# Expert stage of a mixture-of-experts layer: VectorE writes the odd group's first bias row, GpSimd makes the scatter indices

## The reference

```
h  = x @ W1[e].T + b1[e]            # 512 numbers
a, b = split(h, 2)                  # 256 each
g  = a * sigmoid(b)
eo = g @ Wo.T + bo
out += eo * comb[e]                 # over the two chosen experts
```

## Time and profile before

| what | value |
|---|---|
| median of 3 runs | 716.66 us (714.81 to 716.93) |
| the profiled execution, its own time | 718.54 us |
| its span, first to last instruction | 716.8 us |
| granted TensorE clock, mean | 0.949 |
| instructions | 14297 |

### The profile page before, as it was taken

One profiled execution on the slowest core, in us unless ns is written; L12 is line 12 of the kernel. 1 busy time (PEld: TensorE's weight loads), 2 busy tenths in 40 slices (PEclk: granted clock), 3 DMA queues, 4 the chain that ended last, 5 costly groups with the idle time before them and its releaser, 6 DMA issues. The chain is left out here.

```text
span 716.8 us, 14297 instructions
## 1 busy us (share of the span) xinstructions
PE 618.1 (86%) x3515; PEld 470.7 (66%) x3515; DVE 602.6 (84%) x1384; ACT 522.4 (73%) x1321; POOL 536.9 (75%) x657
## 2 busy tenths in 40 slices
PE   3566789999999989989889777828999999999994
PEld 1433556667777667666667465615888888888883
DVE  6389999999999999997999846566788888888884
ACT  2666578898888957986856576644778878887883
POOL 5457667899999779899969884566588766666666
PEclk9989999999999999999999999957999999999997
DMA  4999888889998897898898799625465444444430
GB/s 109 259 140 133 118 115 134 134 141 157 153 139 155 132 139 121 149 169 148 156 148 151 142 266 290 246 97 152 130 98 86 81 82 81 76 84 80 83 60 1
DMA packets 103300, 95.58 MB, mean 133 GB/s; under 512 B 14523, under 2 KB 82710, under 8 KB 102966
## 3 DMA queue, kind: packets, MB, share of 16 engines
q1 hardware_dynamic: 85846, 79.69, 60.3%
q0 software_dynamic: 16176, 12.75, 9.6%
q10 hardware_dynamic: 1200, 2.23, 0.8%
HBM read 35.47 MB, written 25.61 MB: 85 GB/s over the span
## 5 line engine op out<-in xcount | busy, mean ns | idle before, releaser
L2065 POOL DMA_INDIRECT out<-res,index x91 | 141.4, 1553 | 56.4 <-DVE res L2150 36.5
L843 POOL TENSOR_TENSOR rs_prod<-rT,state_rows 128x512 f32<-128x512 f32 x128 | 139.3, 1097 | 41.0 <-DVE state_rows L1528 39.3
L1281 PEld LDWEIGHTS ps_k<-w,gel 128*128 128x128 f32 x512 | 61.4, 200 | 17.0 <-issue 13.2
L1989 ACT ACTIVATE sig<-ps_a 128x256 f32<-128x256 f32 x91 | 35.1, 385 | 42.8 <-DVE glu L2126 16.9
L1281 PE MATMUL ps_k<-w,gel 128*128 128x128 f32 x512 | 64.1, 286 | 2.4 <-ACT gel L1098 2.4
L1246 PE MATMUL ps_f<-hnT_hi,mix_hi 128*128 128x512 f32 x128 | 55.2, 431 | 8.4 <-DVE hnT_lo L1651 7.6
L2117 DVE SCALAR_TENSOR_TENSOR half<-ps_b,xg,sig 128x256 f32<-128x256 f32 x91 | 43.6, 479 | 21.4 <-ACT sig L1993 18.6
L2110 DVE SCALAR_TENSOR_TENSOR ps_a<-ps_a,xg,sig 128x256 f32<-128x256 f32 x91 | 44.4, 487 | 11.0 <-issue 7.5
L2015 ACT ACTIVATE ps_b<-bias_rows 128x512 f32 x89 | 53.0, 595 | 0.0
L1248 PE MATMUL ps_f<-hnT_hi,mix_lo 128*128 128x512 f32 x128 | 52.2, 408 | 0.0
L1247 PE MATMUL ps_f<-hnT_lo,mix_hi 128*128 128x512 f32 x128 | 52.1, 407 | 0.0
(11 more groups left out here) (357 smaller groups left out, 2000.6 us busy)
## 6 DMA issues: line engine op xcount, KB each, us to landing
v_spread<-vT SPq DMA_DIRECT2D x128, 256.0 KB, 5.3
xg<-sorted_scratch SPq DMA_DIRECT2D x91, 130.0 KB
xin<-in_L_attn_x SPq DMA_DIRECT2D x16, 256.0 KB, 6.3
x<-in_L_attn_x SPq DMA_DIRECT2D x16, 256.0 KB
out<-x SPq DMA_DIRECT2D x16, 256.0 KB
sorted_scratch<-gel SPq DMA_DIRECT2D x4, 910.0 KB, 8.0
tokens_scratch<-h SPq DMA_DIRECT2D x12, 256.0 KB
raw_w<-in_L_ffn_W ACTq DMA_DIRECT2D x2, 1024.0 KB, 9.3
```

Source lines behind the costliest of these rows:

```text
L843: pool.tensor_tensor(rs_prod[:, p, idx % 4], rT[p][:], state[idx][:, p * NT:(p + 1) * NT], ALU.mult).then_inc(s["rs_ready"], 1)
L1281: mm = pe.matmul(ps_k2[:, q * P:(q + 1) * P], gel[c][:, q * P:(q + 1) * P], w2[:, c, :], start=(c == 0), stop=(c == NF - 1))
L2065: pool.indirect_dma_start(out_rows, bass.IndirectOffsetOnAxis(ap=index[k % RESULTS][:, i:i + 1], axis=0), res[k % RESULTS][:, i, :], None, ...
```

## The change

VectorE, in its iteration `k`, reads the low expert of group 2k + 3 from `pair_table` into a register at the head of the iteration (`low_of`), and after `join(2k+1)` copies that expert's bias row into the bank `ps_a` of the odd group 2k + 3 (`odd_seed`). TensorE then no longer does the bias product for odd groups from the fourth on, but waits for the copy (`odd_seeded`). GpSimd makes the row numbers of two pairs at once (`number`) into one tile `index`, before the scatters of every second iteration, with waits for the input (`xT_ps`) and for the older scatters (`stored`); `finish` on VectorE no longer makes them.

```diff
-                if j < FIRST_SEED or i == 1:
+                if j < FIRST_SEED:
                     bias(ps_a[j % 2], low)
+                elif i == 1:
+                    pe.wait_ge(s["odd_seeded"], k - FIRST_SEED // 2 + 1)
                 else:
                     pe.wait_ge(s["low_seeded"], k - FIRST_SEED // 2 + 1)
...
             def scatter(k, i):
                 j = 2 * k + i
                 pool.wait_ge(s["res_ready"], k + 1)
+                pool.wait_ge(s["numbered"], k // 2 + 1)
...
+            def number(m):
+
+                first, end = 4 * m, min(4 * m + 4, GROUPS)
+                n, columns = end - first, slice(first % (2 * RESULTS), first % (2 * RESULTS) + end - first)
+                for k in range(2 * m, (end + 1) // 2):
+                    pool.wait_ge(s["xT_ps"], k + 1)
+                    if k >= RESULTS:
+                        pool.wait_ge(s["stored"][k % RESULTS], 16 * count_to(k - RESULTS, RESULTS))
+                rows = xg[:, slot(first):slot(first) + n, TAGS + ID:TAGS + ID + 1].rearrange("p i c -> p (i c)")
+                if first >= early_groups:
+                    left = left_out[:, first - early_groups:end - early_groups]
+                    if first == early_groups:
+                        pool.wait_ge(s["left_set"], 1)
+                    pool.tensor_tensor(left, rows, left, ALU.add).then_inc(s["summed"], 1)
+                    pool.wait_ge(s["summed"], m - early_groups // 4 + 1)
+                    rows = left
+                pool.tensor_copy(index[:, columns], rows).then_inc(s["numbered"], 1)
...
             for k in range(PAIRS):
+                if k % 2 == 0:
+                    number(k // 2)
                 if k >= 1:
                     scatter(k - 1, 0)
                     scatter(k - 1, 1)
...
+            def low_of(j):
+
+                if not FIRST_SEED <= j < GROUPS:
+                    return None
+                if j == early_groups + 1:
+                    dve.wait_ge(s["tables_set"], 1)
+                both = dve.value_load(pair_table[0:1, j:j + 1], min_val=0, max_val=(E - 1) * H2 * (PACK + 1))
+                return (both & (PACK - 1)).with_bounds(min_val=0, max_val=(E - 1) * H2)
+
+            def odd_seed(j, low):
+
+                if FIRST_SEED <= j < GROUPS:
+                    dve.wait_ge(s["glu_ready"], j - 1)
+                    dve.tensor_copy(ps_a[j % 2][:], bias_rows[:, bass.ds(low, H2)]).then_inc(s["odd_seeded"], 1)
...
-                number = xg[:, first:first + n, TAGS + ID:TAGS + ID + 1].rearrange("p i c -> p (i c)")
-                if 2 * k < early_groups:
-                    dve.tensor_copy(index[k % RESULTS][:, 0:n], number)
-                else:
-                    late = 2 * k - early_groups
-                    if late == 0:
-                        dve.wait_ge(s["left_set"], 1)
-                    dve.tensor_tensor(index[k % RESULTS][:, 0:n], number, left_out[:, late:late + n], ALU.add)
...
             for k in range(PAIRS):
+                low = low_of(2 * k + 3)
                 low_half(2 * k)
                 high_half(2 * k)
...
                     join(2 * k + 1)
+                odd_seed(2 * k + 3, low)
```

More of the change, by code:

```diff
@@ L1826, in expert_block @@
         gT = [sb(f"gT{i}", [P, NH2, 2 * P]) for i in range(2)]
-        index = [sb(f"index{i}", [P, 2], I32) for i in range(RESULTS)]
+        index = sb("index", [P, 2 * RESULTS], I32)
+        assert early_groups % 4 == 0 and LOADS % 2 == 0 and RESULTS % 2 == 0
         res = [sb(f"res{i}", [P, 2, P]) for i in range(RESULTS)]
@@ L1837, in expert_block @@
             "small_in parts_set xT_ps xT_hi_ready xT_lo_ready a_ps b_ps sig_a_ready sig_b_ready half_ready glu_a glu_b glu_ready "
-            "gT_ps gT_ready y_ps biased res_ready lo_set listed table_step tables_set left_set low_seeded seeded "
+            "gT_ps gT_ready y_ps biased res_ready lo_set listed table_step tables_set left_set low_seeded odd_seeded numbered summed seeded "
             "route_step gain_ready exps_ready totals_ps totals_ready ranks_ps tag_step").split(),
@@ L2064, in scatter @@
                 pool.wait_ge(s["res_ready"], k + 1)
-                pool.indirect_dma_start(out_rows, bass.IndirectOffsetOnAxis(ap=index[k % RESULTS][:, i:i + 1], axis=0), res[k % RESULTS][:, i, :], None,
+                pool.wait_ge(s["numbered"], k // 2 + 1)
+                pool.indirect_dma_start(out_rows, bass.IndirectOffsetOnAxis(ap=index[:, j % (2 * RESULTS):j % (2 * RESULTS) + 1], axis=0), res[k % RESULTS][:, i, :], None,
                                         bounds_check=TILES * NT - 1, oob_is_err=False, compute_op=ALU.add).then_inc(s["stored"][k % RESULTS], 16)
+            def number(m):
[14 more added lines that the diff above has]
+                pool.tensor_copy(index[:, columns], rows).then_inc(s["numbered"], 1)
             def list_front():
```

## The result

| kernel | median, us | runs |
|---|---|---|
| before | 715.73 | 4 (712.87 to 716.93) |
| changed | 763.82 | 4 (761.37 to 767.08) |

The changed kernel takes 1.068 times as long, with a 95% interval from 1.062 to 1.074: 48.1 us more. The forecast was 767, 50 us more than a median of 716.7. The profiled execution's span went from 716.8 to 759.7, which is 42.9. Part of the difference to 48.1 lies ahead of this stage: its first `low_half` is at 493.13 before and at 489.06 after. From the first `low_half` to the last (705.20 before, 747.90 after) it is 212.07 and 258.85, 46.8 more. The start of the stage differs from trace to trace: over the twelve traces of this case its first even `join` lies between 490.6 and 497.5, so a few microseconds between two profiled executions arise ahead of it.

What follows compares the result with a forecast made beforehand. The prediction took a slackless VectorE-ScalarE ring of 4.62 us a pair as the bound. Additions of 0.33 + 0.59 - 0.08 + 0.32 = 1.16 us over 43 pairs give 50 us, so 767 us; 8-in-10 range 743 to 782.

Steps and rivals of the forecast that it cites:

- the step of 1.54 us: From even `join` on VectorE over ScalarE's `low_seed` and `high_gate` to the next odd `high_half`: 1.54 us of each pair.
- the ring: VectorE and ScalarE in turn, 3.08 + 1.54 = 4.62 us a pair without slack; additions cost in full; 0.68 for 755 to 782.
- The copy: VectorE's bias copy behind the odd `join`: +0.33 us a pair for its later start, +0.59 for its length.
- The term of -0.08: `index`, the row numbers, leaves VectorE ahead of `res`: 0.08 us less a pair.
- The load: Register load on VectorE's sequencer between `res` and even `low_half`: a gap of +0.32 us a pair, bounds 0 to 0.5.
- GpSimd: `number` before the scatters every second pair, some 0.6 us, covered by 1.21 us of idle time: cost zero.
- The count: 44 copies, of which the first falls where VectorE idles anyway: 43 pairs by 1.16 us, 50 us.
- The four terms: Additions per pair on VectorE: 0.33 copy start, 0.59 copy length, -0.08 `index`, 0.32 load; sum 1.16 us.
- TensorE as the bound: Rival: TensorE sets the pace, so the bias product removed is worth 14 us, about 703 us; chance 0.05.
- VectorE alone as the bound: Rival: waits for ScalarE close and VectorE runs without pause, 4.98 us a pair, about 732 us; chance 0.06.
- The clock: Rival: TensorE, less busy, is granted 1.2 GHz for stretches, 10 us and more on top, over 782 us; chance 0.05.

Runs made afterwards that it cites:

- e1: Kernel before, without TensorE's bias product for odd groups from the fourth on and nothing in its place: ratio 0.9997 to before.
- e5: Changed kernel with two ScalarE calls exchanged, the odd group's `high_gate` before `low_seed`: ratio 1.0246 to before, median 731.42 us.
- e6: Kernel before, without VectorE's two output-bias operations a pair: ratio 0.9948 to before, period 4.59 us.
- e3: Changed kernel without `number`: VectorE loads the expert, copies the bias and still makes `index` itself; ratio 1.0669 to before.
- e4: Changed kernel with VectorE's register load moved between the odd group's `low_half` and `high_half`: ratio 1.0465 to before, median 753.72 us.
- e2: Kernel before with only the row numbers moved to GpSimd (`number`); TensorE keeps its product, VectorE neither loads nor copies: ratio 0.9962 to before.
- e9: Changed kernel, output bias and `res` of pair k-2 moved between even `join` and odd `low_half`, two output banks, early register load: ratio 1.0019 to before.
- e11: Changed kernel with both `high_gate` before `low_seed` on ScalarE and the register load before the odd `high_half`: ratio 1.0198 to before, median 729.15 us.
- e7: Kernel before, without VectorE's output-bias operations and without TensorE's bias product for odd groups: ratio 0.9900 to before, period 4.50 us.
- e8: Kernel before, row numbers on GpSimd, output bias and `res` of pair k-2 between even `join` and odd `low_half`, two output banks: ratio 1.0004, median 714.72 us.

## Why the prediction was right

**The bound.** That VectorE and ScalarE set the pace in a closed ring, and not TensorE, is shown by e1 (the product gone, no gain), e5 (two calls of ScalarE exchanged, 32 us back) and the step of 1.54 us, which is the same in both kernels. The prediction took "whatever is taken from TensorE alone gives nothing" from three rows of VectorE without idle time and one wait. Its margin was thin, which it didn't say: e6 shows TensorE's own pace at 4.59, so the ring led by 0.03 to 0.05. It also passed over the odd `low_gate`, which ends 0.02 ahead of `low_seed` in the earlier trace rows and comes from TensorE; only e1 shows that the `join` was what held it. The rule that whatever is added to the ring costs in full didn't depend on this margin, and it held.

**The copy.** Its start was forecast at 0.67 behind the `join` and is at 0.62: the own wait and register work cost +0.28, not +0.33. The register operations are 40 and 46 ns on VectorE and 35 and 53 on ScalarE, so there was nothing to scale: the wait is 0.20 on both. Its length was forecast at 0.67 and is 0.695. It is slower still than the two-input operation of its size (0.674), so the shorter time of the cast (0.421) wasn't to be had here. The sentence of the Trainium skill (VectorE: DVE Perf Modes, Why PSUM operands drop a tier), by which an operand in PSUM keeps float32 at one element a cycle, agrees with these 0.695. In the ring it is +0.61, not +0.59.

**`index`.** The term of -0.08 appears in the step table. But e3 shows that it is not a term by itself: in a kernel with the load at the head, `index` stands under the load. The two terms were -0.08 and +0.32; together they are +0.22 to +0.23 with `index` and without it.

**The load.** +0.30 where +0.32 was forecast, shown by e4. The load itself took 301 ns. The floor of about 600 ns that the Trainium skill gives for `tensor_load` (DMA: Bandwidth & Descriptors, Latency and other measured facts) is neither the load's time here nor what it cost; from `res` to the end of the check it is near 0.6, of which `res` covered half.

**GpSimd** was costed at zero and cost zero: e3 without `number` isn't faster than the changed kernel. The two operations take 0.98 us and not 0.4, still under the cover of GpSimd's idle time. In e2, where the pairs are shorter, 20 scatters between 515 and 700 us wait for the row numbers, 12.3 us in all, and the period doesn't show it.

**The count.** 43 pairs by 1.16 were 50; by the measured 1.14 they are 49, and the medians are 48.1 apart. That they meet so well is in part luck. The four terms are off by 0.05 at most and cancel in part, and the stage itself grew by 46.8: its first four periods, which are longer than the ring in both kernels, add up to 20.76 before and 23.40 after, 2.6 more and not 4.6.

**The rivals.** TensorE as the bound fell by e1. VectorE alone as the bound was a case that the changed kernel isn't in. e9 is, at 4.61. e5 has the 4.98 that the rival gave and no wait of VectorE for ScalarE, but the ring of e11 lies at most 0.04 under it, so its figure isn't VectorE's alone. The clock did not fall, with TensorE busy for 83% of the stretch.

**What isn't settled:** the third ring of e7 and the one of e11, which are read from rows and not tested, and how much of the 4.5 us between the medians of e6 and e8 the longer end of e8 (2.9 us in the traces) explains.

**A version that beats both**, by little, is e2: 0.4% (0.1 to 0.6), the row numbers on GpSimd and nothing else of the change. Its period is shorter by 0.04 to 0.06 us, which is 1.7 to 2.6 us or 0.2 to 0.4% by itself.

## What to carry to other kernels

A busy row at 100% and a chain that names one engine don't prove a bound: walk one period of the next busiest engine and look for a stretch without idle time that ends in a wait for another engine's queue, since such a ring may close with no slack. Taking work out of an engine and putting nothing in its place is one cheap run that tells it, and it should come before the work is given to another engine. The register load at the head of VectorE's loop cost the 0.3 us that the instruction ahead of it didn't cover, and nothing where the sequencer waits anyway (e4); look for such a place first.

## What the runs showed of the hardware

VectorE's copy of 128x512 float32 from SBUF to a PSUM bank took 695 ns, more than ScalarE's 595 to 602 for the same. A register load took 301 ns on VectorE's sequencer and 282 on ScalarE's; the register operations behind it took 190 and 152. GpSimd's sum of 128x4 took 0.79 us here and a cast of 128x4 from `xg` 0.77, where a cast of the same size from `work` has a mean of 186 ns and a 128x4 operation earlier in the kernel one of 203; the slow ones are those that read `xg`. A VectorE operation that waits for the one ahead of it started 0.09 us behind its end, or 0.20 with register operations for a run-time address in between, and one without a wait 0.08 before its end.
